# The sequence stage of a chunked state-space block rewritten: 32x64 score tiles, one scan a pair, one bank for the late part, new orders

## What is computed

```python
scores = einsum('bcihn,bcjhn->bcijh', Cc, Bc) * Lm * dtc        # C B^T inside a chunk, causal, with decays
y_intra = einsum('bcijh,bcjhp->bcihp', scores, xc)
chunk_state = einsum('bckhn,bckhp->bchnp', Bc, wx)
h, = scan: h = chunk_decay * h + chunk_state                    # carry over 32 chunks
y_cross = einsum('bcthn,bchnp,bcth->bcthp', Cc, h_states, exp(dAcs))
y = y_intra + y_cross + xp * D_param; y = y / rms(y) * norm_w * silu(z); out = y @ W_out.T
x = layernorm(x + out)
logits = -|x - keys|^2 + x @ rw.T + rb; topv, topi = top_k(logits, 4); w = softmax(topv)
```

## Time and profile before

| | us |
|---|---|
| median of 3 runs | 387.39 (385.04 to 388.74) |
| profiled execution, first to last instruction | 314.5 |
| TensorE busy | 283.4 (90%) |
| ScalarE busy | 209.2 (67%) |
| VectorE busy | 204.3 (65%) |
| POOL busy | 143.7 (46%) |

### The profile page before, as it was taken

The page is one execution under the profiler, slowest core; times in us unless marked ns, Lnnn a source line. Parts: engine busy times, 40 slices in busy tenths (PEclk is TensorE's granted clock), DMA queues, the critical chain, the costliest instruction groups (busy, mean ns, idle before and its releaser), DMA issues.

```text
span 314.5 us, 10587 instructions
## 1 busy us (share of the span) xinstructions
PE 283.4 (90%) x2948; PEld 250.6 (80%) x2949; DVE 204.3 (65%) x914; ACT 209.2 (67%) x725; POOL 143.7 (46%) x146
## 2 busy tenths in 40 slices
PE   2999899999999997899889899999999999997591
PEld 2986668687677775799779899999999999995480
DVE  2237768898888888866888566555655566641272
ACT  1475466575574743577667688888888889885064
POOL 1200000657456474777677775555555564424000
PEclk9979999999999999599999999999999999999697
DMA  6999920111111111342122232222222222100884
GB/s 212 300 336 374 415 95 2 40 39 57 38 58 48 39 58 47 87 103 78 48 83 90 80 92 72 65 81 71 67 69 67 70 68 60 42 12 6 305 273 92
DMA packets 25260, 33.30 MB, mean 106 GB/s; under 512 B 4299, under 2 KB 18020, under 8 KB 24832
## 3 DMA queue, kind: packets, MB, share of 16 engines
q1 hardware_dynamic: 20432, 23.30, 24.7%
q0 software_dynamic: 4352, 8.79, 7.9%
q10 hardware_dynamic: 432, 0.67, 0.7%
HBM read 21.76 MB, written 11.50 MB: 106 GB/s over the span
## 4 chain that ended last, share of the span: by engine, by line
PE 70%; DVE 11%; DMA 6%; issue 5%; ACT 5%; POOL 1%; DVEq 1%; POOLq 0%; ACTq 0%; SPq 0%
PE bank L774 16%; PE bank L752 15%; PE bank L747 4%; PE bank L539 4%; PE bank L553 4%; DMA yrows<-shared,idi 3%; PE bank L844 3%; PE bank L764 3%; PE bank L530 2%; PE bank L736 2%; PE bank L514 2%; PE bank L591 2%; DMA small<-in_small 2%; PE bank L601 2%; PE bank L563 2%
## 5 line engine op out<-in xcount | busy, mean ns | idle before, releaser
L1881 POOL DMA_INDIRECT yrows<-shared,idi x72 | 75.9, 1054 | 56.1 <-ACT shared L1790 32.6
L1860 POOL DMA_INDIRECT xrows<-rows_all,sli x64 | 62.4, 975 | 81.6 <-issue 63.4
L1769 ACT ACTIVATE shared<-bank,shared 128x128 f32<-128x128 f32 x256 | 73.2, 370 | 19.1 <-PE bank L752 19.1
L752 PE MATMUL bank<-shared 128*128 128x128 f32 x512 | 70.0, 281 | 2.5 <-issue 2.5
L774 PE MATMUL bank<-w2s,shared 128*128 x512 | 68.1, 276 | 0.8 <-DVE shared L1464 0.4
L752 PEld LDWEIGHTS bank<-shared 128*128 128x128 f32 x512 | 63.8, 196 | 3.9 <-issue 3.8
L774 PEld LDWEIGHTS bank<-w2s,shared 128*128 128x128 f32 x512 | 62.3, 192 | 1.4 <-issue 1.4
L1450 DVE COPY shared<-w1s 128x644 f32 x64 | 33.1, 517 | 28.5 <-issue 27.7
L1790 ACT ACTIVATE shared<-shared,idg 128x128 f32<-128x128 f32 x72 | 29.9, 418 | 7.1 <-DVE shared L1464 5.8
L1641 ACT ACTIVATE shared<-bank,small 128x256 f32<-128x256 f32 x64 | 25.1, 476 | 4.7 <-PE bank L539 4.7
L965 DVE TENSOR_TENSOR shared<-bank,small 128x512 f32<-128x512 f32 x32 | 21.2, 682 | 1.3 <-PE bank L553 1.3
(11 more groups left out here) (221 smaller groups left out, 472.0 us busy)
## 6 DMA issues: line engine op xcount, KB each, us to landing
shared<-xrows SPq DMA_DIRECT2D x64, 70.0 KB
w1s<-in_w1T SPq DMA_DIRECT2D x1, 4128.0 KB, 24.5
w2s<-in_w2T SPq DMA_DIRECT2D x1, 4096.0 KB, 22.9
w1s<-yrows SPq DMA_DIRECT2D x8, 512.0 KB, 7.9
yrows<-shared,idi POOLq DMA_INDIRECT x72
xrows<-zrow SPq DMA_DIRECT2D x1, 1120.0 KB, 13.9
xp_all<-in_xp SPq DMA_DIRECT2D x1, 1024.0 KB, 7.8
w1s<-in_b SPq DMA_DIRECT2D x1, 1024.0 KB, 20.9
```

The source lines that it names most:

```text
L752: m = mm(hidden_bank(u)[:, f * P:(f + 1) * P], w[:, f * P:(f + 1) * P], xbT[u][:, :], start=True, stop=True)
L1769: m = act(hT[u][:, f * P:(f + 1) * P], hidden_bank(u)[:, f * P:(f + 1) * P], ACT.Gelu, bias=w[:, F + f:F + f + 1])
L1860: po.indirect_dma_start(out=xrows, out_offset=bass.IndirectOffsetOnAxis(ap=sli[:, g, k:k + 1], axis=0), in_=rows_all[:, g, :], in_offset=N ...
L1881: po.indirect_dma_start(out=yrows, out_offset=bass.IndirectOffsetOnAxis(ap=idi[r][:, 0:1], axis=0), in_=yw[r][:, :], in_offset=None, bound ...
```

## The change

- Scores: tiles of 32 rows by 64 columns (two heads instead of four), 16 products of 128 columns a tile of tokens into banks 3, 4, 6 and 7; block_diag needs two passes instead of four.
- States: eight products a tile on four column tiles of 32, only the blocks that are needed, a pair's states side by side. new_states multiplies them by the factors, and carry is one scan over 160 elements a pair instead of eight operations; states_out on ScalarE (four copies of 32 partitions) puts them back into block form. The factors are laid out by POOL (chunk_factors), ahead of its first send.
- project makes x alone and turns B back from project_cb's result by two transposes.
- y_cross and y_back work on a pair, the halves of the columns taking turns; y_intra has its own half bank (bank 5, upper half), and skip_products adds there.
- The residual and the router ride in out_product: x @ [I, keys] + y @ [W, W keys], 144 columns; x2_transpose, x2_copy and router are gone. normed is on ScalarE (rows_normed) for pairs 0 to 5.
- positions takes the bf16 one-hot choices directly, 20 products; a running base replaces count_chosen, counts and early_counts.
- The late part lies in one bank, 1, instead of two.
- New orders in the loop, on each engine; y_cross, y_back and skip of a pair, place, slots and gates come one step later than before. Loads: x by tokens goes (1 MB), W_out and an identity come (64 KB each).

The diff, cut to its core:

```diff
+CP = 2 * NC
+HR = H // 8
+ZG = 4
+NZ = -(-NT // ZG)
+DE = D + 16
...
-        late = (bank[6], bank[1])
...
+        psum = {k: ctx.enter_context(nc.psum_tensor(f"bank{k}", [P, 512 * len(k)], F32)) for k in ("0", "1", "2", "34", "5", "67")}
+        bank = [psum[k][:, i * 512:(i + 1) * 512] for k in ("0", "1", "2", "34", "5", "67") for i in range(len(k))]
+        score_banks = (3, 4, 6, 7)
...
             def project(t):
...
+                pe.wait_ge(s1["cb_act"], t + 1)
+                mm(bank[0][:, 0:D], xT_all[:, t * P:(t + 1) * P], winT[:, 0:D], start=True, stop=True)
...
+                for j in range(2):
+                    m = pe.transpose(bank[0][:, (j + 1) * P:(j + 2) * P], cb[t % 4][:, 2 + j, :], ident)
+                m.then_inc(s1["pj_mm"], 1)
...
+                after(s1["ds_dve"], (t + 1) // 2)
                 c_ = cb[t % 4]
                 for j in range(2):
                     for q in range(NC):
...
+                        for r, b in enumerate(score_banks):
+                            rows = slice(r * HR * NS, (r + 1) * HR * NS)
+                            m = mm(bank[b][q * Q:(q + 1) * Q, j * P:(j + 1) * P], c_[rows, 2 + j, q * Q:(q + 1) * Q],
+                                   cbd[t % 2][rows, j, q, :], start=True, stop=True, skip_group_check=True)
                 m.then_inc(s1["sc_mm"], 1)
 
             def states(t):
...
                 pe.wait_ge(s1["b_act"], t + 1)
...
+                after(s1["ds_dve"], t // 2)
+                for g in range(2 * H // 4):
+                    j, r = divmod(g, 4)
+                    to = states_at[r * HR * NS:(r + 1) * HR * NS, j * Q:(j + 1) * Q].rearrange("p (a s x) -> p a s x", a=2, s=2)
+                    m = mm(to[:, :, t % 2, :], bs[t % 2][:, g * 32:(g + 1) * 32],
+                           xz[t % 4][:, g * 32:(g + 1) * 32].rearrange("p (a x) -> p a x", a=2), start=True, stop=True, skip_group_check=True)
+                m.then_inc(s1["st_mm"], 1)
+
+            def y_cross(m_):
...
+                pe.wait_ge(s1["e_act"], m_ + 1)
+                pe.wait_ge(s1["cb_act"], 2 * m_ + 2)
+                pe.wait_ge(s1["yit_act"], 2 * m_ + 2)
                 for j in range(2):
...
+                    for q in range(NC):
+                        for s in range(2):
+                            m = mm(bank[5][s * Q:(s + 1) * Q, q * D + j * 64:q * D + (j + 1) * 64],
+                                   cb[(2 * m_ + s) % 4][:, j, q * Q:(q + 1) * Q], hs[m_ % 2][:, s * NC + q, j, :],
+                                   start=(j == 0 and q == 0), stop=False, skip_group_check=True)
+                m.then_inc(s1["yc_mm"], 1)
...
+            def y_back(m_):
                 pick = ident.rearrange("p (c z q w) -> p q c z w", c=4, z=2, q=NC)[:, :, :, 0, :]
...
+                pe.wait_ge(s1["yit_act"], 2 * m_ + 2)
                 for a in range(4):
...
+                    for s in range(2):
+                        y = bank[5][s * Q:(s + 1) * Q, 0:NC * D].rearrange("p (q a c w) -> p q a c w", q=NC, a=4, c=4)
+                        m = mm(y[:, :, a, :, :], yiT[s][:, a * Q:(a + 1) * Q], pick, start=False, stop=(a == 3),
+                               skip_group_check=True)
                 m.then_inc(s1["y_mm"], 1)
 
...
+            def y_transpose(m_):
...
+                pe.wait_ge(s1["yg_dve"], m_ + 1)
+                after(s1["base_dve"], m_)
                 for q in range(NC):
...
+                    m = pe.transpose(late[:, q * D:(q + 1) * D], yg[m_ % 2][:, q, :], ident)
                 m.then_inc(s1["yt_mm"], 1)
 
             def out_product(m_):
...
                 pe.wait_ge(s1["yt_act"], m_ + 1)
                 for q in range(NC):
...
+                    mm(late[:, q * DE:(q + 1) * DE], xTp[:, 2 * m_ + q, :], idkw[:, :], start=True, stop=False)
+                    m = mm(late[:, q * DE:(q + 1) * DE], yT[m_ % 2][:, q, :], woutn[:, :], start=False, stop=True)
                 m.then_inc(s1["wo_mm"], 1)
...
 
             def positions(m_):
...
+                pe.wait_ge(s1["oh_dve"], m_ + 1)
...
                 for q in range(NC):
...
+                    for k in range(TOPK):
+                        mm(late[:, 288 + q * E:288 + (q + 1) * E], before[:, :], oh[m_ % 2][:, q, k, :], start=(k == 0),
+                           stop=(q == 0 and k == TOPK - 1))
+                for k in range(TOPK):
+                    mm(late[:, 288 + E:288 + 2 * E], ones16[:, :], oh[m_ % 2][:, 0, k, :], start=False, stop=(k == TOPK - 1))
+                for q in range(NC):
+                    for k in range(TOPK):
+                        m = mm(late[:, 320:320 + E], ones16[:, :], oh[m_ % 2][:, q, k, :], start=(q == 0 and k == 0),
+                               stop=(q == 1 and k == TOPK - 1))
                 m.then_inc(s1["pos_mm"], 1)
...
             for s in range(1, NP):
+                tile(scores, 2 * s - 2, first=2)
+                pair(y_cross, s - 2, first=0)
+                pair(skip_products, s - 2, first=0)
+                pair(y_back, s - 2, first=0)
+                tile(project_cb, 2 * s, first=4)
+                tile(states, 2 * s - 1, first=3)
+                tile(y_intra, 2 * s - 2)
+                pair(positions, s - 3)
+                tile(scores, 2 * s - 1)
                 tile(project, 2 * s, first=2)
-                tile(project_cb, 2 * s, first=4)
-                tile(scores, 2 * s - 1)
                 pair(y_transpose, s - 2)
-                tile(y_cross, 2 * s - 2)
-                tile(y_cross, 2 * s - 1)
+                tile(project_cb, 2 * s + 1, first=3)
                 pair(out_product, s - 2)
-                tile(y_intra, 2 * s - 2)
-                tile(scores, 2 * s, first=2)
-                if s == EARLY + 2:
-                    early_counts()
                 tile(project, 2 * s + 1, first=3)
-                pair(x2_transpose, s - 2)
                 tile(states, 2 * s, first=2)
-                pair(router, s - 2)
                 tile(y_intra, 2 * s - 1)
-                tile(project_cb, 2 * s + 1, first=3)
-                tile(states, 2 * s + 1, first=3)
-                tile(y_back, 2 * s - 2)
-                tile(y_back, 2 * s - 1)
-                if s == EARLY + 2:
-                    pe.wait_ge(c1, 1)
-                pair(skip_products, s - 1)
-                pair(positions, s - 2)
...
+            def new_states(m_):
+                ve.wait_ge(s1["st_mm"], 2 * m_ + 2)
...
+                tt(chunk_states(m_)[:, :, :, 1:CP + 1].rearrange("p a w c -> p a c w"),
+                   states_at.rearrange("p (a c w) -> p a c w", a=4, c=CP),
+                   gmx[:, m_, :].rearrange("p (a w c) -> p a c w", a=4, w=HD)[:, :, 1:CP + 1, :], ALU.mult).then_inc(s1["ds_dve"], 1)
+
+            def carry(m_):
+                ve.wait_ge(s1["ds_dve"], m_ + 1)
+                at_m = hx[:, CP * m_:CP * m_ + 4 * HD * (CP + 1)]
+                ve.tensor_tensor_scan(at_m, gmx[:, m_, :], at_m, 0.0, ALU.mult, ALU.add).then_inc(s1["h_dve"], 1)
...
+            def next_base(m_):
+                now = c("ebase") if m_ == 0 else base[m_ % 2][:]
+                tt(base[(m_ + 1) % 2][:], late[:, 320:320 + E], now, ALU.add).then_inc(s1["base_dve"], 1)
...
+                pair(new_states, s - 1, first=1)
+                pair(place, s - 3)
+                pair(gated, s - 2)
+                tile(causal1, 2 * s - 1)
+                tile(take_x, 2 * s, first=2)
+                pair(gates, s - 3)
+                tile(causal0, 2 * s - 1)
+                pair(carry, s - 1, first=1)
+                pair(res_stats, s - 2)
+                pair(res_moments, s - 2)
+                pair(slots, s - 3)
+                tile(take_x, 2 * s + 1, first=3)
+                pair(square_sums, s - 2)
+                pair(neg_means, s - 2)
+                pair(key_bias, s - 2)
+                pair(logits, s - 2)
+                tile(causal1, 2 * s)
+                tile(causal0, 2 * s)
+                pair(best, s - 2)
+                pair(y_scale, s - 1)
+                pair(below_best, s - 2)
+                pair(y_add, s - 1)
                 pair(best_ids, s - 2)
                 pair(one_hot, s - 2)
...
+            def states_out(m_):
...
+                ac.wait_ge(s1["h_dve"], m_ + 1)
+                after(s1["yc_mm"], m_ - 1)
+                for r in range(4):
+                    rows = slice(r * HR * NS, (r + 1) * HR * NS)
+                    m = act(hs[m_ % 2][rows, :, :, r * 2 * HD:(r + 1) * 2 * HD],
+                            chunk_states(m_)[rows, :, :, 0:CP].rearrange("p (j a) w c -> p c j (a w)", j=2), cp)
+                m.then_inc(s1["e_act"], 1)
...
+            def rows_normed(m_):
+                ac.wait_ge(s1["nm_dve"], m_ + 1)
+                ac.wait_ge(s1["lg_dve"], m_ + 1)
+                for q in range(NC):
+                    m = act(rows_all[:, 2 * m_ + q, 0:D], out_rows(q), ACT.Identity, scale=rv[m_ % 2][:, q:q + 1],
```

(13 more changed lines are left out.)

670 lines of the change are left out of this document (299 added, 371 removed).

## The result

| | before | changed |
|---|---|---|
| median of 20 runs each, us | 387.04 (385.04 to 391.29) | 391.27 (386.57 to 394.85) |
| ratio | | 1.0081 (1.0052 to 1.0109) |
| profiled execution, first to last instruction | 314.5 | 389.3 |

The changed kernel is 0.8% slower, where 374.1 us (3.4% faster) was forecast.

A forecast was written before the change was run, and what follows sets the result against it. TensorE was taken to set the 12.86 us step, with POOL's 10.1 us a pair as floor. Pair 6 through at 55.9 + 4 x 10.5 + 3 x 10.1 = 128.2, not 141.48: 387.39 - 13.3 = 374.1 us, range 368.5 to 383.0.

The forecast's parts named there:

- 72.9 lie around the span: Whole run: the median 387.39 exceeds the profile's span 314.5 by 72.9 us, taken as outside the span and unchanged.
- the same code: Expert stage behind the sends: its blocks, pair 7's scatters and tail stay as they were, shifting earlier by 13.3 us.
- TensorE's sum: TensorE's pieces in one loop step, priced one by one: 9.9 us against 12.86 before.
- the 10.5 forecast: Length of a loop step: 10.5 us, between POOL's floor of 10.1 and 11.6.
- my rival at 11.6: Rival: the serial round of the one late bank makes steps 11.6 us; gain 6.4, 381.0 us, chance 0.21.
- The rule of the Trainium skill on 60 cycles a product: TensorE overhead per matmul: scores 0.80 instead of 0.60, states 0.40 instead of 0.29, sum 10.5 instead of 9.9; not adopted.
- VectorE and ScalarE: Their work in one loop step after the change: 9.1 us each, under TensorE's 9.9 and POOL's 10.1.
- the slower rival: Rival: chunk factors on POOL ahead of the first send cost up to 25 ns an element; 401 us, chance 0.08.
- The first send: POOL's first send at 55.9 us: step 2 starts near 36.1, step 3 near 45.5, the send some 10.4 into it.
- my own sum: End of pair 6's sends: 55.9 + 4 x 10.5 + 3 x 10.1 = 128.2 us, against 141.48 before.
- the 13.3 us of gain: Earlier end of pair 6's sends, 128.2 for 141.48, carried whole into the run time.
- my rival "no change": Rival: VectorE and ScalarE take over at 12.5 us or more a step; about 386 us, chance 0.06.

The follow-up runs named there:

- b0_before_again: The kernel before, unchanged, profiled once more with the span of every execution; 387.6 us in the profiled run, span 385.7.
- a_late: The changed kernel with all 56 sends of the loop held back until pair 5 is ready; 389.8 us, ratio 0.996 to before.
- a_gap8: The changed kernel with a POOL memset of 8 elements behind each send of pairs 0 to 5; 315.1 us, before 314.76 in that session.
- a_mask: The changed kernel with one-hot choices first summed on VectorE into a mask, 5 products in positions instead of 20; 312.4 us, ratio 0.992.
- a_early_gap2: The changed kernel with ids packed and slots earlier, plus two POOL memsets of 140 elements behind each send; 336.9 us, ratio 1.064 (before 315.62).
- a_early: The changed kernel with ids packed right behind gate_exp and slots right behind gates, nothing else; 391.9 us, ratio 1.003.
- after_again: The changed kernel, unchanged, run again beside before; 390.8 us, ratio 1.007.
- b_late: The kernel before with all 56 sends of the loop held back until pair 5 is ready; 396.2 us, ratio 1.016.

## Why the prediction was wrong

**The step that failed first** is "so 72.9 lie around the span; I leave them". They don't: wherever a run has both its span and its time, they are 1.8 to 2.3 us apart. The Trainium skill, Runtime: NRT & Kernel Launch, section The ~15µs preamble/postamble breakdown, puts launch and end together at 9 to 15 us. That should have made 72.9 suspect; the 1.8 to 2.3 measured here lie below the page's figure too, and decide. All that I read from the first profile was true of an execution that the timed runs were not: 314.5 us go with steps of 12.8 us, the timed 387 with steps of 21.9, as b0_before_again shows. The gain was then taken from a POOL and a TensorE that never stood in each other's way, "the same code" behind the sends included, which with hold-up took 191.9 us from pair 6's end in b0_before_again for 173.0 in the first profile.

**TensorE's sum** was right where it can be seen, between the start of the loop and the first send:

```profile
51.10 0.69 PE L576 MATMUL bank<-shared 32*64 32x128 f32 x32
52.35 0.69 PE L603 MATMUL bank<-hs,shared 128*64 128x64 f32 x16 [0.56 <-ACT yiT L1596]
52.97 0.71 PE L641 MATMUL bank<-wxd,xTp 128*128 128x128 f32 x4
53.61 0.69 PE L632 MATMUL bank<-cst,yiT 128*64 128x64 f32 x16
54.58 1.13 PE L561 MATMUL bank<-xT_all,winT 128*128 128x128 f32 x8 [0.28 <-issue]
55.64 0.33 PE L589 MATMUL bank<-xz,bs 128*32 128x32 f32 x16
55.78 0.63 PE L622 MATMUL bank<-shared,xz 128*16 128x64 f32 x32
56.35 0.36 PE L675 MATMUL bank<-oh,before 128*128 128x16 bf16 x8
...
56.94 0.69 PE L576 MATMUL bank<-shared 32*64 32x128 f32 x32
57.56 0.49 PE L548 MATMUL bank<-winT,xT_all 128*128 128x128 f32 x2
...
58.32 1.06 PE L561 MATMUL bank<-xT_all,winT 128*128 128x128 f32 x8
59.22 0.41 PE L661 MATMUL bank<-idkw,xTp 128*128 128x144 f32 x2
...
61.56 0.69 PE L576 MATMUL bank<-shared 32*64 32x128 f32 x32
```

Scores 0.62 (0.60 forecast), y_cross 0.62 (0.60), y_back 0.69 (0.60; 0.97 to the next piece, less its idle of 0.28), states 0.14 (0.29), positions 0.59 (0.52), out product 1.02 (1.13); the step, 51.10 to 61.56, is 10.46 us for the 10.5 forecast, so the one late bank's round, my rival at 11.6, did not bite. The rule of the Trainium skill on 60 cycles a product (TensorEngine Tiling (Array Packing), Performance Considerations) had 0.80 and 0.40 for scores and states: the trace doesn't agree for small tiles side by side.

**VectorE and ScalarE**: a_late's stage gives 15.91 and 16.95 of 20 us, so 8.4 and 8.9 us in a step of 10.6, for 9.1 and 9.1. The scan of 160 elements took 0.48 (0.45), and POOL's factors were done at 35.0: the slower rival fell, a power's price was not theirs.

```profile
59.58 0.48 DVE L956 TENSOR_TENSOR_SCAN hx<-gmx,hx 128x160 f32<-128x160 f32 x1
```

```profile
33.30 1.71 POOL L1862 COPY gmx<-gm 128x160 f32<-128x160 f32 x4
```

**The first send** was forecast at 55.9 and came at 66.16. Step 3 began at 51.10, not 45.5: 5.6 us, of which 4.5 were there when step 2 began (40.62 for 36.1) and 1.1 came in step 2 (10.5 for 9.4). Slots ended where I had them, 10.6 us into the step. Then the send waited for the ids, which ScalarE packs late in its list, at 64.92: 4.5 us that I had left out of what a send waits for (the row of 88.76 above names it, "<-ACT rows_all L1643"). The stretch from 35 to 40 us, the changed kernel by stage and in TensorE's order of time, then before by stage:

```profile
35.00:40.00 5.00, 3.91 (x45) 3.21 (x48) 1.45 (x3) 1.60 (x4) 0.02 (x1) 0.50 0.76 324
```

```profile
35.45 2.05 PE L561 MATMUL bank<-xT_all,winT 128*128 128x128 f32 x8 [0.31 <-issue]
```

```profile
35.00:40.00 5.00, 4.44 (x71) 3.82 (x70) 3.54 (x10) 2.59 (x7) 0.00 (x0) 1.00 1.03 437
```

The changed kernel was granted 0.50 there, the 1.2 GHz level, and one project_cb (L561) took 2.05 us for 1.06 to 1.13 later; before stood at 1.00, 2.4 GHz. The changed kernel's granted clock was 0.61 from 20 to 35 us as well. TensorE had waited 1.05 us for ScalarE at 20.6 and 1.62 for VectorE at 30.4. I had costed step 1 by what it no longer holds, as if the clock were given; how the 4.5 us divide between the clock and these waits is not shown.

With 66.2 for 55.9 my own sum gives 66.2 + 4 x 10.5 + 3 x 10.1 = 138.5 for the end of pair 6, and without hold-up a_gap8 had 139.4, against 141.5 of before: of the 13.3 us of gain 2 are left at that place and none in the time (315.1, one run, beside 314.8); a_mask, the nearest other kernel, had 138.9 and 312.4, 0.8% under before. So the change would in all likelihood have missed its forecast without hold-up too. That a late start costs what it is late is shown by a_early_gap2 up to the end of pair 6, at spaced sends; at sends 1.27 us apart a_early met only a session with hold-up, and the changed kernel itself was never run without. Both stay open.

**With hold-up** the chain is: step of before 12.8 without and 21.9 with (56.16 to 143.72 in four), of the changed kernel 10.5 and 22.3 (66.16 to 155.40). Before hides 1.0 us of its step in the 10.1 us of the burst, the changed kernel loses 1.7 us on top of the burst. The fallen clock is part of this: from 100.25 to states at 105.94 TensorE needed 5.7 us for what had taken 3.9 ahead of the first send (56.94 to 60.85, less three of 32 instructions). Before pays for it too, with 0.50 up to 94. Against the second profile of before the first send is 10.0 us later, pair 6 is through 7.8 us later (201.6 for 193.8) and the span ends 3.6 later: all seven pairs' steps together gave 2.2 us back, where 13 and more were forecast, and what lies behind pair 6 gave 4.2. Neither number is firm: after_again sends first at 64.4, is through with pair 6 at 198.3 and has 191.4 us behind it, as much as before. The changed kernel's TensorE work by time shrank, its instructions grew (a_late's 492 matmul instructions in 20 us are 260 a step, b_late's 280 are 180). One explanation is that instructions are what is short in a burst. It fits that the changed kernel got 32 of them from 90.09 to 100.25, tiny ones for the most part, and a_early again 32, mostly larger ones of scores, from 79.37 to 89.39; before got only some 16 in its burst, so it isn't one fixed number. The one edit meant to test it, the mask, was run without hold-up, and with hold-up only where positions lay outside the burst, so it is an explanation and not a finding. The result lies near my rival "no change", but not for its reason: neither VectorE nor ScalarE took over.

## What to carry to other kernels

Compare the span with the times before anything is costed: where they differ by more than the few microseconds that lie around a span, the profile is of another condition than the times, and a sum from its rows is a sum for that condition. List for each transfer all that it waits for, with the place of each in its engine's queue, ids and other small copies too. And where POOL issues many indirect DMAs back to back, try them further apart: 0.36 us more from send to send bought 46 us here, or cost 18, by the condition (0.1 us bought 4).

## What the runs showed of the hardware

- Bursts of POOL's indirect DMAs (128 rows of 560 B, one each 1.27 us) can hold up the issue of TensorE and ScalarE for most of the burst: 20 tiny products took 7.0 us for 0.6, the 16 products of one scores call 9.2 for 0.62, and a copy of ScalarE stood 5.8 us with its input there. At 1.37 us apart little of it goes, at 1.63 most. POOL's memsets of 1.1 us do nothing of the sort.
- After such a burst TensorE's granted clock stood at 0.50 for some microseconds more, in both kernels: until 104 us where the burst ended at 98.6, until 94 where it ended at 88.7.
- Whether it happens goes with the session, not with the kernel: before took 387 to 390 us in five sessions and 315 in two, and one chip number was seen with both. What differs between these sessions no run here shows, nor which path the instructions are held up on. The Trainium skill, Runtime: NRT & Kernel Launch, section Instruction fetch mechanics, holds that the refilling of the engines' instruction memories is mostly hidden; whether these are what comes late, no run here shows.
